# Fused cross-attention on Trainium2: the query weights arrive in blocks cut by x's features instead of by column blocks

## The reference

```
memory_proj    = memory @ W_mem^T                       # (1024, 512)
scores         = x @ memory_proj^T / sqrt(512)          # (512, 1024)
attn           = softmax(scores)
memory_context = attn @ memory_proj                     # (512, 512)
gate           = sigmoid([x, memory_context] @ W_gate^T + b_gate)
fused          = x + gate * memory_context
out            = fused * rsqrt(mean(fused^2) + 1e-6) * norm_w
```

## Time and profile before

| | us |
|---|---|
| median of 3 runs | 117.36 (117.07 to 117.45) |
| the profiled execution's own time | 116.81 |
| its span | 115.0 |

### The profile page before, as it was taken

The page is one execution under the profiler, slowest core; times in us unless marked ns, Lnnn a source line. Parts: engine busy times, 40 slices in busy tenths (PEclk is TensorE's granted clock), DMA queues, the critical chain, the costliest instruction groups (busy, mean ns, idle before and its releaser), DMA issues.

```text
span 115.0 us, 1528 instructions
## 1 busy us (share of the span) xinstructions
PE 108.6 (94%) x501; PEld 89.8 (78%) x501; DVE 70.9 (62%) x105; ACT 68.1 (59%) x114; POOL 28.1 (24%) x30
## 2 busy tenths in 40 slices
PE   7999999999999999999999999999999999999900
PEld 7887888888888888888888888888878888888800
DVE  0499969997998358000459759998472011366891
ACT  4398959999634658330958487694373402147741
POOL 1000000000000008792492000690059000036640
PEclk9999999999999999999999999999999999999999
DMA  2999998769998999970000497899960400003604
GB/s 63 323 364 383 293 390 284 254 251 301 238 311 203 224 301 272 398 268 6 0 0 3 182 312 193 280 292 217 259 256 21 182 0 0 6 8 140 217 16 166
DMA packets 13975, 22.64 MB, mean 197 GB/s; under 512 B 1552, under 2 KB 6416, under 8 KB 13968
## 3 DMA queue, kind: packets, MB, share of 16 engines
q1 hardware_dynamic: 13536, 21.93, 60.1%
q10 hardware_dynamic: 432, 0.62, 1.8%
HBM read 16.25 MB, written 6.29 MB: 196 GB/s over the span
## 4 chain that ended last, share of the span: by engine, by line
PE 86%; DVE 4%; ACT 3%; issue 2%; POOL 2%; POOLq 1%; ACTq 0%
PE wide L845 19%; PE wide L808 19%; PE wide L864 18%; PE wide L760 10%; PE wide L875 6%; PE wide L892 5%; PE wide L824 5%; PE wide L746 4%; DVE gate L629 2%; DVE gate L622 2%; ACT gate L454 1%; ACT squares L463 1%; POOL res L391 1%; POOLq L29 1%; DVE gate L616 1%
## 5 line engine op out<-in xcount | busy, mean ns | idle before, releaser
L391 POOL TENSOR_TENSOR res<-gate,vecs 128x512 f32<-128x512 f32 x7 | 8.5, 1208 | 34.6 <-DVE gate L629 27.4
L377 POOL TENSOR_TENSOR ctxT_lo<-ring,ctxT_hi 128x512 fp32r<-128x512 f32 x4 | 5.6, 1417 | 43.4 <-ACT ctxT_hi L414 43.4
L606 DVE TENSOR_TENSOR wgT_lo<-wide,wgT_hi 128x512 fp32r<-128x512 f32 x4 | 2.7, 688 | 18.8 <-ACT wgT_hi L450 18.8
L808 PE MATMUL wide<-ctxT_hi,qT_lo 128*128 128x512 f32 x32 | 12.5, 390 | 0.0
L808 PE MATMUL wide<-ctxT_hi,qT_hi 128*128 128x512 f32 x32 | 12.5, 390 | 0.0
L808 PE MATMUL wide<-ctxT_lo,qT_hi 128*128 128x512 f32 x32 | 12.5, 389 | 0.0
L426 ACT ACTIVATE probs<-wide,neg_max 128x1024 f32<-128x1024 f32 x8 | 8.9, 1109 | 3.5 <-DVE neg_max L574 3.3
L574 DVE TENSOR_REDUCE neg_max<-wide 128x1 f32<-128x1024 f32 x8 | 9.7, 1212 | 1.9 <-PE wide L808 1.8
L432 ACT ACTIVATE probs<-probs,inv_sum 128x1024 f32<-128x1024 f32 x8 | 9.2, 1148 | 0.7 <-DVE inv_sum L579 0.7
L864 PE MATMUL wide<-wgT_lo,xT_hi 128*128 128x512 f32 x32 | 8.6, 389 | 0.0
L864 PE MATMUL wide<-wgT_hi,xT_lo 128*128 128x512 f32 x32 | 8.6, 389 | 0.0
(11 more groups left out here) (90 smaller groups left out, 246.7 us busy)
## 6 DMA issues: line engine op xcount, KB each, us to landing
ring<-ctxT SPq DMA_DIRECT2D x8, 256.0 KB, 4.9
ring<-w_gateT SPq DMA_DIRECT2D x8, 256.0 KB, 5.3
ring<-ctxN SPq DMA_DIRECT2D x8, 256.0 KB, 7.1
xr<-x_rows SPq DMA_DIRECT2D x8, 256.0 KB, 4.9
ring<-passage SPq DMA_DIRECT2D x16, 128.0 KB, 4.0
out<-res SPq DMA_DIRECT2D x7, 256.0 KB, 2.0
ring<-xT SPq DMA_DIRECT2D x6, 256.0 KB, 6.8
passage<-spare SPq DMA_DIRECT2D x3, 512.0 KB, 3.5
```

The source lines that it names most:

```text
L391: nc.gpsimd.tensor_tensor(res[:, j % 2], gate[:, j % 2, 1:], gain, ALU.mult)\
L808: last = nc.tensor.matmul(sums("scores", j, h), qT_s[left][:, c, rows], ctxT_s[right][:, c, cols], start=(c == 0 and (left, right) == (HI, ...
```

## The change

The blocks of W_mem are cut the other way: a block now holds *both* column blocks c for *one* feature block k. It is still 128 KB in 128 partitions by 256 elements, there are still four, and they stand at the same places of the list (W_mem, x, W_mem, x, ...). The host's array is the same, so a block's 256 elements are now two runs of 512 bytes for each partition. The passes of k = 0 and k = 1 are issued by kinds, both column blocks in each kind, in place of the two orders written by hand. The 24 passes, the loads' sizes and everything behind them stay.

```diff
-        def wm_block(c, half):
-            ks = slice(half * KD // 2, (half + 1) * KD // 2)
-            block(("wm", c, half), w_mem[:, c, ks], wm_s, c, ks)
+        def wm_block(k):
+            block(("wm", k), w_mem[:, :, k], wm_s, slice(None), k)
...
-        wm_block(0, 0)
-        xT_block(0, 0)
-        wm_block(1, 0)
-        xT_block(0, 1)
-        wm_block(0, 1)
-        xT_block(0, 2)
-        wm_block(1, 1)
-        xT_block(0, 3)
+        for k in range(KD):
+            wm_block(k)
+            xT_block(0, k)
...
-                wm_i, xT_i = index_of["wm", c, 2 * k // KD], index_of["xT", b, k]
+                wm_i, xT_i = index_of["wm", k], index_of["xT", b, k]
...
-            def first_queries():
-
-                query_pass(0, 0, 0, (HI, HI))
-                query_pass(0, 0, 0, WITH_LO_OF_W)
-                query_pass(0, 1, 0, (HI, HI))
-                query_pass(0, 0, 0, WITH_LO_OF_X)
-                query_pass(0, 1, 0, WITH_LO_OF_X)
-                query_pass(0, 1, 0, WITH_LO_OF_W)
-
-            def second_queries():
-                for c in range(KE):
-                    query_pass(0, c, 1, (HI, HI))
-                    query_pass(0, c, 1, WITH_LO_OF_W)
-                for c in range(KE):
-                    query_pass(0, c, 1, WITH_LO_OF_X)
+            def first_queries(k):
+
+                for kind in ((HI, HI), WITH_LO_OF_W, WITH_LO_OF_X):
+                    for c in range(KE):
+                        query_pass(0, c, k, kind)
...
-            first_queries()
-            second_queries()
+            for k in range(KD // 2):
+                first_queries(k)
```

## The result

The changed kernel takes 117.95 us (median of 19 runs, 117.35 to 118.89) against 117.1 us of the kernel before (19 runs, 116.64 to 117.86): a ratio of 1.0073 with a 95% interval of 1.0052 to 1.0094, or 0.6 to 1.1 us more. The forecast was 117.5 us in a range of 117.0 to 118.3, with a chance of 0.24 for a loss of more than 0.35 us.

What follows compares the result with a forecast made beforehand. PE was taken to bound the kernel, unbroken from the first warm-up matmul to 99.57 us. Order (-0.03 us) plus packets (+0.20) gave +0.17 us on 117.36, so 117.5 us, range 117.0 to 118.3.

Steps and rivals of the forecast that it cites:

- its likeliest case: Whole kernel: +0.05 to +0.32 us, likeliest time 117.5 us, chance 0.48 with the fourth rival counted in.
- What bounds the kernel: PE's unbroken run to 99.57 us: gains or losses in its first ten microseconds reach the end in full.
- The order of the passes: First query passes: pass 7 wins 0.24 us, pass 18 waits for DVE and gives back 0.21, leaving -0.03 us.
- the fourth rival: Query passes: pass 7 stays near 6.8 us because x's second block comes later; time and chance counted with the forecast.
- The price of a packet: DMA engines before x's last block: 32 further packets each at 6 ns, +0.20 us; bounds 0 to 28 ns.
- From there on all is as before: Everything after pass 18, forecast to start at 9.29 against 9.32 us: no further change expected from the order of passes.
- I cost the second run at nothing: SP's issues of weight loads: some 0.43 us each, no added cost; far end 1.07 us each, x's last block issued 2.6 later.
- The rival that came true: Landing of x's blocks before pass 18: packets decide from 12 ns each; +0.87 us, 118.2, at 28 ns; chance 0.24.

Runs made afterwards that it cites:

- The kernel with one run: The changed kernel with each weight block laid out as one run of 1 KB per partition instead of two of 512 bytes: 117.05 us, ratio 0.9993 to before.
- the kernel before with two runs: The kernel before, its W_mem blocks laid out as two runs of 512 bytes per partition: ratio 1.0070 to before, 1.0042 when timed again.
- changed blocks, old passes: The changed kernel's loads with the passes in the order of the kernel before: 118.01 us, ratio 1.0072 to before.
- x in two runs: The kernel before with the four x blocks of batch 0 in two runs of 1 KB per partition: 117.97 us, ratio 1.0062 to before.
- the last three blocks: The changed kernel with its first weight block in one run, only the other three in two of 512 bytes: 118.69 us, ratio 1.0109 to before.

## Why the forecast held in its range and missed in its likeliest case

**What bounds the kernel: right, but for 0.2 us.** The loss arises in the first 13 us, and all but 0.23 us of it reaches the end. The forecast said that no later slack could swallow anything; the 48 passes at 85.50 us were such a slack.

**The order of the passes: right.** The forecast said that pass 7 comes earlier, that pass 18 gives it back behind DVE's low part of x, and that -0.03 us are left. The kernel with one run shows it, and its ratio is 0.9993. In the changed kernel itself pass 7 came at 7.14 instead of 6.58, since the weights and x's second block were late; the fourth rival had this and rightly gave it no price of its own.

**The price of a packet: slightly small, and not all of its term.** Forecast 6 ns, measured 8 to 10 ns: 32 of them are 0.26 to 0.33 us instead of 0.20. The forecast had read 44 against 90 ns as a hint that it might be nothing; its 90 ns is a mean with a few long packets in it, the usual 2 KB packet of the kernel before took 84. x's last block landed at 3.97 + 4.2 = 8.17 us, 0.42 later than 7.75, and pass 18 stood 0.41 later. The size fits, but packets are not shown to be its cause: the kernel with only its first weight block in two runs has 8 further packets an engine, 0.08 us, and there x's last block was copied at 8.23, as late as in the change. What the two share is the late first weight block and the thin stream at 3.0 to 3.5 us (105 and 133 GB/s against 254), a term that the forecast put at nothing when it cost the second run only by its packets. From the Trainium skill (DMA: Bandwidth & Descriptors, "Why small descriptors are slow") the forecast had an estimate of 4 ns; the trace, with 8 to 10 ns, does not agree in size.

**"From there on all is as before": wrong, and this is the step that failed.** The forecast followed the stream only to x's last block. It took the loads behind as hidden, having noted for the kernel before that the engines are full from 3 us on. In both profiles of the changed kernel the second memory block, two loads further, landed 1.8 to 2.2 us later than before, and PE had nothing to do between queries and scores. A slack that I never worked out was exceeded: before, that block was copied at 9.28 us, just in front of the high part of the queries at 9.82, on ACT, which both pass in order; the queries' part was done at 10.40, and PE was free for it at 10.92. Some 0.5 us was all the room.

**"I cost the second run at nothing" for SP: wrong in size.** The changed kernel's issues took 0.6 us each instead of 0.43 (SP was done with x's last block at 4.56, 1.1 us later than before), also those of plain loads behind one in two runs. In 1.9 to 2.4 us the kernel before moved 81 packets of SP's queue, the changed one none. In the kernel before with two runs, however, issues took 0.43 to 0.48 us and 110 packets of that queue moved, and there was a loss as well: so slower issues are not needed for it.

**The rival that came true** by its sign and size (+0.85 us, where it had +0.87 at 28 ns a packet) is the second, but not by its mechanism: the packets cost 10 ns, under the 12 from which it was to decide. Its chance of 0.24 was too low, because only the price of packets fed it; the queue's behaviour with a form of load that no row showed deserved more than a word. That 117.95 lies in the range is luck: the upper bound of 118.3 was set by dear packets, and what filled it was a gap that the forecast did not know.

**Open.** Why the stream starts thin, and why it has gaps of 0.5 to 2 us while loads are outstanding. The five profiles with a gap (the change twice, "changed blocks, old passes", x in two runs, the last three blocks) each have four to six packets of more than 0.8 us between 4 and 12 us; of the other nine, one has a single such packet and eight have none. Five of these nine also have loads in more than one run, so such loads do not bring a gap each time. The size of the pieces, their number and the order of passes have been excluded as what decides whether there is a loss; the queue has not. Whether a load in several runs reaches the engines in another way than one in a single run, and why a packet then takes 1 us, nothing here looks into.

## What to carry to other kernels

When a load's cut is changed, keep each partition's part one run in memory: lay out the host's array after the new cut, or the price of the pattern may be higher than the gain. Take more than one profile before a loss of under 1% is explained by one: here single executions differed by 0.7 us at a place that the change doesn't touch. Where one engine takes transfers and results in one written order, a late transfer holds up results that are ready; work out the slack of every load for some blocks past the last one that the change touches. A new order of passes in front of an operand that is just in time gains nothing until that operand comes earlier.

## What the runs showed of the hardware

The usual packet took 27 ns for 512 bytes, 46 for 1 KB and 84 for 2 KB; as means over a full stream it was 27, 44 and 90. Yet four loads in two runs for each partition cost more than their packets say: 0.6 to 0.8% of this kernel, for weight blocks in runs of 512 bytes or in four of 256, and for x's blocks in runs of 1 KB (0.4% in one repeat). The first such load landed not 3.1 but 4.2 us after its issue (4.5 in the kernel before with two runs, 4.8 with four). And in five of the ten profiles with such loads the DMA stream had a gap with loads outstanding, down to 115 to 209 GB/s for 0.5 to 2 us, at places that changed from kernel to kernel (4.5 to 5.0 us, 7 to 9 us, 8.5 to 9.5 us), each with single packets of 0.8 to 1.5 us. From 4.5 to 11 us no half microsecond of the four profiles with all loads in one run was below 266 GB/s.
